# Routed expert tiles on TensorE: gate and up contracted in three slices of 64 rows, with the waits of a tile moved ahead of the down product before it

## The reference

```python
g = jnp.einsum('nh,shi->sni', x, shared_wg)
u = jnp.einsum('nh,shi->sni', x, shared_wu)
shared_out = jnp.einsum('sni,sih->snh', jax.nn.silu(g) * u, shared_wd).mean(axis=0)
...
ge = jnp.einsum('nh,ehi->eni', x, wg)
ue = jnp.einsum('nh,ehi->eni', x, wu)
ye = jnp.einsum('eni,eih->enh', jax.nn.silu(ge) * ue, wd)
routed_out = jnp.einsum('ne,enh->nh', combine, ye)
```

## Time and profile before

| | |
|---|---|
| median of 3 runs | 757.97 us (754.09 to 759.02) |
| profiled execution | 751.9 us, span of its instructions 750.4 us |
| PE busy | 721.9 us, 96% of the span |
| PEld, DVE, ACT, POOL busy | 534.3, 302.1, 238.6, 214.1 us |
| chain that ended last, share of PE | 88% |
| routed stage | about 483 to 697 us of the span |

### The profile page before, as it was taken

How to read it: one execution, slowest core, us unless ns; L and a number is a source line. 1 busy time by engine, 2 the same in 40 slices (tenths; PEclk the granted TensorE clock), 3 DMA queues, 4 the chain that set the end, 5 groups by cost and what they waited for, 6 DMA issues and landing times.

```text
span 750.4 us, 17659 instructions
## 1 busy us (share of the span) xinstructions
PE 721.9 (96%) x7212; PEld 534.3 (71%) x7212; DVE 302.1 (40%) x812; ACT 238.6 (32%) x515; POOL 214.1 (29%) x286
## 2 busy tenths in 40 slices
PE   7999899899999999899999999999999999999995
PEld 6447666677687777667546864789789788888654
DVE  1445576666466637634333742112211211111243
ACT  0202443655546546463243001121222122212110
POOL 5537115754132323200010057112112111211363
PEclk9999999999999999999999999999999999999998
DMA  8700000830000000000000045299999999894133
GB/s 304 275 0 2 3 0 2 287 106 3 1 2 14 2 2 14 2 1 12 1 1 12 1 163 204 83 410 372 353 344 372 337 355 379 333 358 169 32 85 84
DMA packets 34289, 102.80 MB, mean 137 GB/s; under 512 B 5034, under 2 KB 20399, under 8 KB 28849
## 3 DMA queue, kind: packets, MB, share of 16 engines
q1 hardware_dynamic: 24272, 70.29, 26.3%
q0 software_dynamic: 9952, 31.60, 11.4%
HBM read 90.66 MB, written 9.83 MB: 134 GB/s over the span
## 4 chain that ended last, share of the span: by engine, by line
PE 88%; DVE 5%; ACT 2%; issue 2%; another core or an unknown queue 1%; DMA 1%; POOL 0%; SPq 0%; DVEq 0%; ACTq 0%; POOLq 0%
PE PS L1625 14%; PE PS L1989 11%; PE PS L2422 9%; PE PS L2302 6%; PE PS L2426 5%; PE PS L2066 3%; PE PS L1863 3%; PE PS L2438 3%; PE PS L1877 2%; PE PS L2390 2%; PE PS L1631 2%; PE PS L2443 2%; PE PS L1903 2%; PE PS L1707 1%; PE PS L1922 1%
## 5 line engine op out<-in xcount | busy, mean ns | idle before, releaser
L1989 PE MATMUL PS<-X,w_sgu 64*128 64x512 f32 x432 | 98.6, 599 | 3.0 <-DVE gu L1457 1.2
L1583 DVE TENSOR_TENSOR rh<-rsg,PS 128x768 f32<-128x768 f32 x32 | 30.5, 955 | 158.3 <-ACT rsg L1021 158.3
L1989 PEld LDWEIGHTS PS<-X,w_sgu 64*128 64x128 f32 x432 | 40.8, 187 | 50.0 <-issue 44.5
L2422 PE MATMUL PS<-xt,w_rgu 128*128 128x128 f32 x576 | 70.1, 276 | 1.0 <-ACT rsg L1021 1.0
L2422 PEld LDWEIGHTS PS<-xt,w_rgu 128*128 128x128 f32 x576 | 67.5, 192 | 3.1 <-issue 3.1
L1021 ACT ACTIVATE rsg<-PS 128x768 f32<-128x768 f32 x32 | 26.0, 811 | 132.5 <-PE PS L2426 101.7
L678 POOL DMA_DIRECT2D y_slots<-ys x32 | 17.6, 551 | 155.2 <-ACT ys L1013 155.2
L1625 PE MATMUL PS<-w_rdn,rh 128*128 128x192 f32 x288 | 50.9, 327 | 0.0
L1625 PEld LDWEIGHTS PS<-w_rdn,rh 128*128 128x128 f32 x288 | 46.2, 190 | 0.4 <-issue 0.4
L832 ACT ACTIVATE pb<-sm,nm 128x128 f32<-128x128 f32 x144 | 42.4, 372 | 10.6 <-DVE nm L1372 10.5
L580 POOL TENSOR_TENSOR rs<-ve,minus_half 128x3 f32<-128x3 f32 x12 | 10.5, 871 | 118.1 <-DVE ve L1283 118.1
(11 more groups left out here) (376 smaller groups left out, 1394.8 us busy)
## 6 DMA issues: line engine op xcount, KB each, us to landing
w_rgu<-in_wgu SPq DMA_DIRECT2D x24, 1152.0 KB, 7.6
w_pgu<-in_wgu SPq DMA_DIRECT2D x16, 1152.0 KB, 7.3
w_rdn<-in_wd POOLq DMA_DIRECT2D x22, 576.0 KB, 6.6
w_pdn<-in_wd POOLq DMA_DIRECT2D x16, 576.0 KB, 6.3
x_slots<-zeros SPq DMA_DIRECT2D x1, 3072.0 KB
xs<-x_slots SPq DMA_DIRECT2D x32, 96.0 KB, 4.5
y_slots<-ys POOLq DMA_DIRECT2D x32, 96.0 KB, 5.8
w_sgu<-in_shared_gu SPq DMA_DIRECT2D x2, 1152.0 KB
```

The costliest lines, as they stand in the source:

```text
L1583: dve.tensor_tensor(rh[:, j, :], rsg[:, j, :], PS[:, 2:4, :].rearrange("p a b -> p (a b)")[:, 0:FF], ALU.mult).then_inc(S["r_h"], 1)
L1989: mm = pe.matmul(PS[:, bank, :], w_sgu[rows, e, c, 128 * m:128 * m + 128], X[rows, c, tokens], start=(c == 0), stop=(c == 2))
L2422: pe.matmul(dst(y, m), w[:, y, 128 * m:128 * m + 128], xt[:, j, y, :], start=(m % 4 == 0), stop=False, skip_group_check=True)
```

## The change

The weights of a routed expert are laid out as those of the shared experts were: in each of three columns a block of 64 inputs of gate in the lower 64 rows, and one of up in the upper 64 (`sides`). ACT therefore makes a third column of turned tokens, with the halves exchanged, in two more copies of 64 rows. A whole tile is then 36 half-height products in one form, a half tile 24 in one form. The waits of the next tile (`tile_ready`: `r_xe`, `r_w`, `r_sg`, `r_h`) are called inside `down`, ahead of its last product, and `turn_hidden` stands ahead of the tile.

```diff
-        xt = tb3("xt", [128, 2, 2, 128])
+        xt = tb3("xt", [128, 2, 3, 128])
...
-                act.activation(xt[:, j, :, :], PS[:, 6 + j, 0:2 * 128].rearrange("p (c t) -> p c t", c=2), ACT.Copy
+                act.activation(xt[0:DR, j, 2, :], PS[DR:128, 6 + j, 128:256], ACT.Copy)
+                act.activation(xt[DR:128, j, 2, :], PS[0:DR, 6 + j, 0:128], ACT.Copy)
+                act.activation(xt[:, j, 0:2, :], PS[:, 6 + j, 0:2 * 128].rearrange("p (c t) -> p c t", c=2), ACT.Copy
                                ).then_inc(S["r_xe"], 1)
...
-                    accumulate(PS[:, 4 + j, 0:D], [(rh[:, j, 128 * m:128 * m + 128], down_weights(k)[:, m, :]) for m in range(FM)]
-                               ).then_inc(S["r_y"], 1)
+                    for m in range(FM):
+                        if m == FM - 1 and ready is not None:
+                            ready()
+                        mm = pe.matmul(PS[:, 4 + j, 0:D], rh[:, j, 128 * m:128 * m + 128], down_weights(k)[:, m, :], start=(m == 0),
+                                       stop=(m == FM - 1))
+                    mm.then_inc(S["r_y"], 1)
...
+            def tile_ready(i, r, k):
+                pe.wait_ge(S["r_xe"], i + 1)
+                pe.wait_ge(S[f"r_w{k}"], r * 16 + 16 if k < FR else r * 32 + 32)
+                if not isinstance(i, int) or i >= 1:
+                    pe.wait_ge(S["r_sg"], i)
+                    pe.wait_ge(S["r_h"], i)
+
+            def whole_tile(j, k):
 
                 w = gate_up(k)
...
+                for c in range(3):
                     for m in range(FM):
...
+                        for y, rows in enumerate(SIDES):
+                            mm = pe.matmul(PS[:, 2 * y + m // 4, 128 * (m % 4):128 * (m % 4) + 128], w[rows, c, 128 * m:128 * m + 128],
+                                           xt[rows, j, c, :], start=(c == 0 and m % 4 == 0), stop=(c == 2), skip_group_check=True)
+                            if c == 2 and m == FM - 1:
+                                mm.then_inc(S[("r_g", "r_u")[y]], 1)
...
             def routed(i, n, j, r, k):
                 static = isinstance(i, int)
-                pe.wait_ge(S["r_xe"], i + 1)
-                pe.wait_ge(S[f"r_w{k}"], r * 16 + 16 if k < FR else r * 32 + 32)
+                if static and i == 0:
+                    tile_ready(i, r, k)
+                if k == 0 and not (static and i == 0):
+                    turn_hidden(i - 1, 1 - j, r - 1)
...
+                following = (lambda: tile_ready(i + 1, r + (k + 1) // RK, (k + 1) % RK)) if not static or i + 1 < RT else None
                 if k >= 1:
-                    down(i - 1, 1 - j, r, k - 1)
+                    down(i - 1, 1 - j, r, k - 1, following)
                 elif not static or i >= 1:
-                    down(i - 1, 1 - j, r - 1, FR)
+                    down(i - 1, 1 - j, r - 1, FR, following)
+                else:
+                    following()
...
-    a["wgu"] = np.ascontiguousarray(np.stack([g[:, 0:DM], u[:, DR:], np.concatenate([u[:, 0:DR], g[:, DM:]], 1)], 2))
+    a["wgu"] = np.stack([sides(i["L0_ffn_wg"][e], i["L0_ffn_wu"][e]) for e in range(E_R)])
```

More of the change, by code:

```diff
@@ L2371, in turn_tokens, with down @@
                 turn_split(PS[:, 6 + j, 0:128], PS[:, 6 + j, 128:256], xs[:, j, :]).then_inc(S["r_xT"], 1)
-            def down(i, j, r, k):
+            def down(i, j, r, k, ready=None):
                 if k >= 2:
@@ L2388, in down @@
                         for h in range(2):
+                            if m == FM - 1 and h == 0 and ready is not None:
+                                ready()
                             at = slice(HALF * h, HALF * h + HALF)
@@ L2407, in _ @@
             pe.wait_ge(S["e_gu"], FM * EARLY + BEFORE)
-            def whole_tile(i, j, k, between):
-                w = gate_up(k)
[L2413 to L2420, removed]
-                    for m in range(FM):
[L2422 to L2436, removed]
-                        for h in range(2):
[L2438 to L2446, removed]
+            def tile_ready(i, r, k):
[4 more added lines that the diff above has]
+                    pe.wait_ge(S["r_h"], i)
@@ new lines, in half_tiles @@
+            def half_tiles(j, k):
+                for c in range(3):
+                    for bank, at in ((0, slice(0, 512)), (1, slice(512, FF))):
+                        for h in range(2):
+                            for y, rows in enumerate(SIDES):
+                                mm = pe.matmul(PS[HALF * h:HALF * h + HALF, 2 * y + bank, 0:at.stop - at.start],
+                                               xt[rows, j, c, HALF * h:HALF * h + HALF], gate_up(k, h)[rows, c, at], start=(c == 0), stop=(c == 2),
+                                               skip_group_check=True)
+                                if c == 2 and bank == 1 and h == 1:
+                                    mm.then_inc(S[("r_g", "r_u")[y]], 1)
@@ L2448, in routed @@
             def routed(i, n, j, r, k):
                 static = isinstance(i, int)
-                pe.wait_ge(S["r_xe"], i + 1)
-                pe.wait_ge(S[f"r_w{k}"], r * 16 + 16 if k < FR else r * 32 + 32)
+                if static and i == 0:
+                    tile_ready(i, r, k)
+                if k == 0 and not (static and i == 0):
+                    turn_hidden(i - 1, 1 - j, r - 1)
                 if k == FR:
-                    half_tiles(i, j, k)
+                    half_tiles(j, k)
@@ L2454, in routed @@
                 else:
-                    whole_tile(i, j, k, (lambda: turn_hidden(i - 1, 1 - j, r - 1)) if k == 0 and not (static and i == 0) else (lambda: None))
+                    whole_tile(j, k)
                 if not static or 0 < i and i + 1 < RT:
@@ L2579, in layout @@
     a["ids"] = np.ascontiguousarray(np.stack([i["itok_BS_0_4999"].T, i["x_txt"].T], 1))
-    g, u = i["L0_ffn_wg"], i["L0_ffn_wu"]
-    a["wgu"] = np.ascontiguousarray(np.stack([g[:, 0:DM], u[:, DR:], np.concatenate([u[:, 0:DR], g[:, DM:]], 1)], 2))
+    a["wgu"] = np.stack([sides(i["L0_ffn_wg"][e], i["L0_ffn_wu"][e]) for e in range(E_R)])
     a["shared_gu"] = np.stack([sides(i["L0_ffn_shared_wg"][e], i["L0_ffn_shared_wu"][e]) for e in range(E_S)])
```

## The result

The changed kernel takes 764.58 us (median of 20 runs, 758.63 to 770.07) against 757.97 (20 runs, 752.89 to 762.51): a ratio of 1.0088, interval 1.0065 to 1.0110. So it is slower by about 0.9%, 6.6 us, where 5.1 was forecast.

The account below looks back on a forecast made before the run. TensorE, busy 96% of the span and waiting for nobody in the routed loop, was taken as the bound. Terms -1.2 + 4.4 + 0.75 + 1.2 = +5.1 us, added to the median 757.97, gave 763.1; range 755.5 to 771.

Parts of the forecast that it names:

- changes of form: Half tiles: one change between full-height and half-height products fewer, 0.15 us each in eight, -1.2 us.
- early waits with the loop's edges: Waits ahead of the last down product: +4.4 us over 23 transitions; at six loop edges +1.2 us.
- first tile: Between tiles 0 and 1, with no down product there, PE stands until rh is done: +0.75 us.
- Whole tiles: Gate and up products of 24 whole tiles: 36 steps of 0.11 us before and after, difference 0.
- rival 2: Whole tiles: half-height pairs hide something and gain; a step 0.01 shorter gives 5.8 us less, 757.3; chance 0.04.
- The handover: Before the last down product: 0.19 us lost (0.15 to 0.21) after tiles 1, 2, 3; 0 after a pass's first.
- The copies: ACT's two added token copies per tile: 0.27 each, overlapping by 0.10, token rows end at 575.46 before rh; cost 0.
- rival 3: ACT's token copies don't overlap, end at 576.00, are waited for last: PE 0.3 later, 31 transitions, +9, 772; chance 0.12.
- Its sign, idle time released by ACT's xt: Idle on PE just before the last down product, released by ACT's xt instead of DVE's rh, would show rival 3.
- The loop's edge: After a pass's last tile, PE's sequencer meets the branch late: 0.2 us (0 to 0.4) at six edges, +1.2 us.
- rival 4: The loop's longer body on PE doesn't stay loaded: instruction fetches add 5 to 23 us, 772 as a middle; chance 0.06.

Follow-up runs that it names:

- second experiment: The kernel before, with old forms and single token copy, only the four waits moved ahead of the last down product: 760.82 us, ratio 1.0133.
- sixth experiment: The changed kernel with waits back at the tile's start, plus eight unused identity products between tiles 0 and 1: 751.32 us, ratio 0.9960 to before.
- fourth experiment: The changed kernel with ACT's two extra token copies made for the first two tiles only, stale rows elsewhere: 756.59 us, ratio 1.0079 to before.
- eighth experiment: The changed kernel, unaltered, run again on the second chip: 765.5 us, ratio 1.0105 to before.
- experiment 5: The changed kernel with the token wait (r_xe) placed last among the four waits: 765.84 us, ratio 1.0138 to before.
- experiments 1, 3: 1: changed kernel, its four waits back at the tile's start, 750.34 us, ratio 0.9999; 3: changed kernel, waits one down product earlier, 767.1 us, ratio 1.0199.

## Why the prediction was right

**Right in the sum.** 763.1 was forecast and 764.58 measured, and the mechanism is in the main the one forecast: the wait ahead of the last down product loses its cover, and each tile pays for it. The second experiment shows it by itself, with 6.1 us for the 5.6 forecast. The sum is a little lucky, since two terms were mis-sized in opposite directions. With the sixth experiment as reference (same forms, no early waits), the stage's 6.95 us are:

| term | forecast | measured |
|---|---|---|
| changes of form | -1.2 | -2.6 (213.59 - 215.49 - 0.73) |
| early waits with the loop's edges | +4.4 + 1.2 | +8.85 (222.44 - 213.59) |
| first tile | +0.75 | +0.73 |

The second term is 3.25 above the forecast, and 2.22 of that are the token copies: without them (fourth experiment) the stage takes 220.22 us.

**Whole tiles: 0, right.** Gate and up products take 4.22 us, 36 pairs of matmuls of 0.112 each and 0.19 for the first load and the step out of the form, where the stages of 2.77 and 1.54 took 4.31; the 0.09 of draining has gone from the middle to the step ahead, as forecast; rival 2 had no part.

**Changes of form: one overlooked.** The half tile takes 4.03 us (forecast 4.05), 0.165 less. But the tile behind the half tile's down products saves 0.196 too: these are 128x64, and the old form then went to full height and to half height, two changes, where the new form needs one. That this is the reason is my reading; the time is measured. I had counted changes inside the tile and not at its borders. That is the other half of the 0.36 a pass.

**The handover: right to 0.03, but not everywhere.** After tile 1 it is 0.22, where 0.19 was taken (upper bound 0.21). After tile 0 I had put nothing, and the unrolled pass and the kernel without copies show 0.05: nearly right, had there been no more copies.

**The copies: the step that failed.** I had them overlap silu and each other by 0.10, as the old copy did, so that the token rows would end at 575.46, before rh. Groups of ACT in after, by shape:

```profile
L1006 ACT ACTIVATE xt<-PS 64x128 f32<-64x128 f32 x32 | 8.8, 275 | 0.8
L1007 ACT ACTIVATE xt<-PS 64x128 f32<-64x128 f32 x32 | 8.6, 269 | 0.4
L1008 ACT ACTIVATE xt<-PS 128x256 f32<-128x256 f32 x32 | 12.3, 384 | 0.4
```

The length was right (0.27), the overlap was not. In the timeline above the first copy starts when silu is done (558.52, with rh at 558.53) and each next one 0.01 to 0.02 behind the last. Together they last 0.95, exactly as long as rh. So the token rows end within 0.01 of rh, past the point from which rival 3 let them decide (0.18 ahead of rh). In the loop the register steps behind the token wait then follow: 0.18 after tile 0, 0.08 after tile 2, 0.10 after tile 3, 0.35 a pass by the fourth experiment. Rival 3 came true in part: it had put the token rows' end 0.17 behind rh. Its sign, idle time released by ACT's xt, is in the trace (2.7 of the 7.2 us ahead of the down products), but only after tile 1 and in the unrolled passes, just where the copies cost nothing: with two ends 0.01 apart the name of the releaser can't tell the cause. The place after a pass's first tile, where no idle time was forecast, has some.

**The loop's edge: right.** The place after tile 3 costs 0.54 where that after tile 2 costs 0.30; the 0.24 is the branch (forecast 0.2). Only five edges pay it, where six were counted: at the last, where the loop is left, the branch takes 0.08 instead of about 0.22, and the place costs 0.34. Timeline of after at one edge:

```profile
566.36 0.30 PEld L2388 LDWEIGHTS PS<-w_rdn,rh 128*128 128x128 f32 x2 [0.36 <-issue]
566.97 0.64 PEld L2408 LDWEIGHTS PS<-ident,rh 128*128 128x128 f32 x6 [0.32 <-issue]
```

**The first tile: right.** PE stood 0.98 us ahead of tile 1 before, and 1.97 after; timeline of after:

```profile
489.77 0.95 DVE L1585 TENSOR_TENSOR rh<-rsg,PS 128x768 f32<-128x768 f32 x1 [4.43 <-ACT rsg L1023]
...
490.87 4.29 PE L2430 MATMUL PS<-xt,w_rgu 64*128 64x128 f32 x72 [1.97 <-DVE rh L1585]
```

That this idle time can also cost 1.6 us of clock was not in the forecast. It did not in this execution, and did in the eighth experiment's.

**Code: rival 4 had no part.** From 545 to 670 us the DMA view of after shows one packet of instructions:

```profile
q8 instruction: 1, 0.02, 0.0%
```

The store of 2048 instructions that the Trainium skill gives TensorE ("Runtime: NRT & Kernel Launch", Instruction fetch mechanics) agrees: the longer body stays loaded too.

## What to carry to other kernels

A wait moved ahead of work that was queued costs what it no longer covers, in each tile, even when the thing waited for is late by hundredths: about 0.2 us here, for a handover and a load that can no longer run ahead. Compare the ends of everything that such a wait waits for, because a second producer that gets slower by as little as two small copies comes level with the first; and in a loop count the sequencer's register steps behind the release as well. The better form of the tile was worth having (0.36 us a pass); the early wait that came with it spent it more than three times over.

## What the hardware showed that I had not expected

- Small ACT copies out of PSUM (64 partitions x 128 columns, 0.27 us) ran strictly one behind the other, and the first started 0.02 behind the end of silu in every tile. The single 128x256 copy of before started 0.10 ahead of it.
- After the same idle time of 1.97 us ahead of tile 1 (2.08 in experiment 5), the granted clock fell to 0.5 to 0.6 for some 4 us in experiments 1, 3 and 8, and stayed at 1.00 in the first execution of after and in experiments 2, 4 and 5. Filled with products that nobody reads, the place kept its full clock.
- ACT's silu loop paused now and then for up to 5.9 us with no releaser in the profile, in before (once) and after alike. It is the largest thing here that one profile can mistake for the change.
